# Loading the slots' z rows two slots ahead of their residual rows in a routed feed-forward block

## Chip, cores and metric

The kernel runs on one core of one Trainium2 chip. The metric is device time in microseconds (us) of one execution. The median of three runs of the kernel before is 1089.14 us (1087.94 to 1089.94).

## The reference

A macaron block on x of shape (2, 2048, 256), float32: a routed feed-forward at half weight, causal attention with one head of 128, and the same feed-forward once more.

```python
x = x + 0.5 * ffn(layernorm(x))
x = x + attention(layernorm(x))
x = x + 0.5 * ffn(layernorm(x))
# in ffn, after its gated attention-like part:
h = ln(x, ln2_w, ln2_b)
winners = argmax(bids(h), axis=-1)             # one of 3 experts per token
hr = square(relu(h @ K_rwkv[e]))               # experts 0 and 1, hidden width 1024
out_rwkv = hr @ V_rwkv[e]
out_trans = (h @ W1 * sigmoid(state @ W2)) @ W3   # expert 2
return x + onehot(winners) . all_out * scale
```

## The kernel before

The 4096 tokens go through each feed-forward in two parts. Part A (`ffn_a_*`) takes them in 8 groups of 512: norms, gates, bids, the ranking of the tokens by expert, and expert 2. It writes one row of 514 words per token into a table in device memory, `routed_rows`, at the place that the ranking gives it: 256 words z (the normalized input of the experts), the token's index, 256 words of residual, a gate. GpSimd does this with indirect DMAs, "scatters". For the last two groups each row is scattered in halves (`scatter_half`, L863): the first half holds z and the index, the second, "late" half the residual and the gate. In the first feed-forward GpSimd issues the four late scatters of the last group (L901 to L904, `last_halves`, called at L1471) only after it has done slot 0's subtractions; in the second feed-forward they come before slot 0.

Part B (`ffn_b_*`) reads the table in 17 slots of 256 rows (`NSLOT` = 17), each slot with the weights of expert 0 or 1. For slot j:

- SyncE loads z into `slot_z` (256 KB) and the rest of the rows into `slot_row` (258 KB). There are two buffers of each, used in turn (p = j % 2).
- TensorE transposes z with 8 small matmuls: T(j), L1227. ScalarE copies the result to `shT_hi` (L1325), VectorE subtracts to get `shT_lo` (L1376). Both are needed by the first product, K(j), 48 matmuls of L407 into `bank` 1 to 4 (36 of them are shown as `bank`, 12 as `banks4to`).
- ScalarE takes relu (L1336) and square (L1344, `hr_hi`), VectorE squares in full precision (L1385, `relu_squared`), GpSimd subtracts (L1451, `hr_lo`), four quarters each.
- V(j), 48 matmuls of L407 into `banks4to`, needs all four quarters of `hr_lo` and, for j > 0, that VectorE has finished the output rows of slot j-1.
- VectorE writes `slot_out` from V(j) and `slot_row` (L1392, L1394; semaphore `orow`), and GpSimd scatters it to the output (L1459).

TensorE's order is T(0), T(1), K(0), K(1), T(2), V(0), K(2), T(3), V(1), K(3), T(4), V(2) and so on (`first` and `body`, L1275 to L1286). VectorE's order inside a slot is: bias of slot j+1 (L1367, L1370), the four squares of slot j, `shT_lo` of slot j+1, output rows of slot j-1. Every engine runs its list in order.

SyncE's order is written out in `ffn_b_sync`. It waits until all scatters but the late ones have landed (L1174), loads z of slots 0 and 1 (L1184), waits for the late halves (L1185), loads the rest of slots 0 and 1 (L1187), and then takes slots 2 to 16 one by one with `slot_in`: wait for T(j-2) to be done, load z(j) (L1179), wait until the output rows of slot j-2 are written (`orow` at least j-1, L1180), load the rest (L1181).

After the first feed-forward all engines meet at a barrier; attention and the second feed-forward follow.

Of the kernel before, what the change touches and what calls it, by code (L numbers as in the profile page):

```python
# [20 lines left out]
BATCH, SEQ, C = 2, 2048, 256  # L21
# [10 lines left out]
NSLOT = N // SLOT + 1  # L32
ROWS = NSLOT * SLOT
ROW = 2 * C + 2
# [17 lines left out]
def hold(eng, sem, value, carrier):  # L52

    if isinstance(value, int) and value <= 0:
        return
    eng.wait_ge(sem, value)
    apart(eng, carrier, value)


def apart(eng, carrier, value):  # L60

    if not isinstance(value, int):
        eng.sem_inc(carrier, 1)


def build_kernel(nc, x, w256, w_st, k_w, v_w, w_qkv, ln, shares, ident, tri, mask, tok, slot_row, pad, out):
    with ExitStack() as ctx:
# [166 lines left out]
        @block.sync  # L234
        def _(sp):
            groups = [one.rearrange("(g t p) c -> g p t c", t=GT, p=P) for one in src]
            setup_sync(sp, b, s, s.ffn[0], groups[0], (ln, ident, w256, w_st, tri, mask, shares, tok, slot_row), pad, b.routed[0])
            ffn_a_sync(sp, b, s.ffn[0], groups[0], s, pad, b.routed[0])
            late_sync(sp, b, s, s.ffn[0], k_w, v_w, w_qkv)
            ffn_b_sync(sp, b, s.ffn[0], b.routed[0])  # L240
            barrier(sp, 1)
            attention_sync(sp, b, a, s.cleared, s.ffn[1], groups[1], pad, b.routed[1])
            ffn_a_sync(sp, b, s.ffn[1], groups[1])
            ffn_b_sync(sp, b, s.ffn[1], b.routed[1])
# [926 lines left out]
def ffn_b_sync(sp, b, f, routed):  # L1171
    c = b.carry["sp"]
    for p in range(2):
        sp.wait_ge(f["scat"][p], 16 * GT * NG // 2)  # L1174
    rg = routed.rearrange("(j t p) c -> j p t c", t=ST, p=P)

    def slot_in(j, p):
        hold(sp, f["sT"], j - 1, c)
        sp.dma_start(b.sz[p][:], rg[j][:, :, 0:C]).then_inc(f["s_in"][p], 16)  # L1179
        hold(sp, f["orow"], j - 1, c)  # L1180
        sp.dma_start(b.srow[p][:, :, 0:ROW - C], rg[j][:, :, C:ROW]).then_inc(f["r_in"][p], 16)  # L1181

    for j in range(2):
        sp.dma_start(b.sz[j][:], rg[j][:, :, 0:C]).then_inc(f["s_in"][j], 16)  # L1184
    sp.wait_ge(f["late"], 16 * GT * 2)  # L1185
    for j in range(2):
        sp.dma_start(b.srow[j][:, :, 0:ROW - C], rg[j][:, :, C:ROW]).then_inc(f["r_in"][j], 16)  # L1187
    with sp.Fori(0, (NSLOT - 3) // 2) as it:
        for par in range(2):
            slot_in(it * 2 + 2 + par, par)  # L1190
    slot_in(NSLOT - 1, 0)

def slots(eng, first, body):
# [910 lines left out]
```

## Time and profile before

| | us |
|---|---|
| median of 3 runs | 1089.14 |
| profiled execution, its own time | 1091.29 |
| its span in the profile | 1089.5 |
| TensorE busy in the span | 1000.6 (92%) |
| TensorE's weight loads busy | 919.8 (84%) |
| VectorE / ScalarE / GpSimd busy | 691.2 / 564.8 / 496.5 |
| mean granted TensorE clock | 0.97 of full |

Slots run from 206.9 to some 437 us in the first feed-forward and from 870 us to the end in the second. In the views, PE is TensorE, PEld its weight loads, DVE VectorE, ACT ScalarE, POOL GpSimd, SPq the queue of SyncE. A timeline row gives start, length, engine, line, operation, what it writes and reads, and in brackets how long the engine stood idle before it and for whom. PEclk is the granted TensorE clock as a share of 2.4 GHz, so 0.50 is 1.2 GHz.

### The profile page before, as it was taken

How to read it: one execution, taken by the hardware profiler on the slowest of the kernel's cores; microseconds unless marked ns; L12 is line 12 of the kernel's file. 1: busy time of each engine (PE TensorE's matmuls, PEld its weight loads, DVE VectorE, ACT ScalarE, POOL GpSimd, SP SyncE). 2: the span in 40 equal slices, each digit the busy share in tenths (PEclk: the TensorE clock that was granted, in tenths of full speed). 3: DMA queues.
4: the chain of work that ended last, by engine and by line, in shares of the span. 5: the costliest groups of instructions: out<-in, count | busy, mean ns of one | idle time of the engine just before them, and what ended most of it. 6: DMA issues, size and time to landing. Idle time of an engine off the chain costs nothing.

```text
span 1089.5 us, 21438 instructions
## 1 busy us (share of the span) xinstructions
PE 1000.6 (92%) x7076; PEld 919.8 (84%) x7077; DVE 691.2 (63%) x1750; ACT 564.8 (52%) x1185; POOL 496.5 (46%) x541
## 2 busy tenths in 40 slices
PE   8999998959999999889988899899999699999997
PEld 7788886959999999778887788678888599999997
DVE  5688877836555554456765668578887764555553
ACT  5776655434454443245553555676664264444552
POOL 3254634456566556551221001135634576556665
PEclk8999998779999999999999999999999799999999
DMA  8621243122111111310222233402212222112211
GB/s 269 200 95 67 90 136 136 59 63 75 59 48 58 58 59 59 100 37 11 87 98 87 78 117 127 145 20 102 75 40 79 78 79 61 58 48 68 77 59 41
DMA packets 51845, 90.01 MB, mean 83 GB/s; under 512 B 5902, under 2 KB 44176, under 8 KB 50576
## 3 DMA queue, kind: packets, MB, share of 16 engines
q1 hardware_dynamic: 43120, 63.64, 18.7%
q0 software_dynamic: 8640, 25.24, 6.2%
q8 instruction: 52, 0.85, 0.3%
q14 instruction: 33, 0.27, 0.1%
HBM read 59.44 MB, written 47.85 MB: 98 GB/s over the span
## 4 chain that ended last, share of the span: by engine, by line
PE 66%; DVE 16%; DMA 6%; ACT 5%; issue 4%; POOL 3%; SPq 1%; DVEq 0%; POOLq 0%; ACTq 0%
PE banks4to L407 32%; PE bank L407 22%; PE banks4to L1694 3%; DMA slot_z<-routed_rows 2%; DVE out_rows L1053 2%; DVE pT_lo L1955 2%; PE bank L1227 2%; PE bank L503 1%; DVE gT_lo L955 1%; PE bank L1706 1%; DVE zT_lo L944 1%; DVE chunk_max L1945 1%; DMA attn_x<-x_after_ffn 1%; PE bank L371 1%; DMA routed_rows<-out_rows,row_index 1%
## 5 line engine op out<-in xcount | busy, mean ns | idle before, releaser
L1385 DVE TENSOR_TENSOR relu_squared<-relu 128x512 f32<-128x512 f32 x136 | 154.9, 1153 | 105.7 <-ACT relu L1336 55.3
L1451 POOL TENSOR_TENSOR hr_lo<-relu_squared,hr_hi 128x512 fp32r<-128x512 f32 x136 | 188.4, 1398 | 59.8 <-DVE relu_squared L1385 55.3
L1336 ACT ACTIVATE relu<-bank,slot_k_bias 128x256 f32<-128x256 f32 x204 | 84.8, 467 | 185.4 <-PE bank L407 168.0
L407 PE MATMUL banks4to<-v_hi,hr_hi 128*128 128x256 f32 x544 | 156.6, 288 | 3.7 <-DVE slot_out L1394 3.0
L407 PE MATMUL banks4to<-v_hi,hr_lo 128*128 128x256 f32 x544 | 153.3, 282 | 0.0
L407 PE MATMUL banks4to<-v_lo,hr_hi 128*128 128x256 f32 x544 | 153.3, 282 | 0.0
L407 PE MATMUL bank<-shT_hi,k_hi 128*128 128x256 f32 x408 | 116.9, 287 | 8.2 <-issue 5.4
L407 PE MATMUL bank<-shT_lo,k_hi 128*128 128x256 f32 x408 | 115.2, 282 | 0.0
L407 PE MATMUL bank<-shT_hi,k_lo 128*128 128x256 f32 x408 | 114.9, 282 | 0.0
L407 PEld LDWEIGHTS banks4to<-v_hi,hr_hi 128*128 128x128 f32 x544 | 103.5, 190 | 7.5 <-issue 7.0
L407 PEld LDWEIGHTS banks4to<-v_hi,hr_lo 128*128 128x128 f32 x544 | 103.5, 190 | 0.0
L407 PEld LDWEIGHTS banks4to<-v_lo,hr_hi 128*128 128x128 f32 x544 | 103.3, 190 | 0.0
L880 POOL DMA_INDIRECT routed_rows<-out_rows,row_index x48 | 48.1, 1001 | 117.6 <-DVE row_index L1036 106.6
L1344 ACT ACTIVATE hr_hi<-relu 128x512 fp32r<-128x512 f32 x136 | 86.1, 633 | 15.9 <-ACT relu L1336 6.9
L407 PEld LDWEIGHTS bank<-shT_hi,k_hi 128*128 128x128 f32 x408 | 76.9, 188 | 11.9 <-issue 11.5
L407 PEld LDWEIGHTS bank<-shT_hi,k_lo 128*128 128x128 f32 x408 | 76.9, 188 | 0.0
L407 PEld LDWEIGHTS bank<-shT_lo,k_hi 128*128 128x128 f32 x408 | 76.6, 188 | 0.0
L1840 ACT CAST pT_hi<-bank 128x512 fp32r<-128x512 f32 (+1 forms) x72 | 39.2, 564 | 55.1 <-PE bank L1706 54.9
L1831 ACT ACTIVATE p<-banks4to,minus_row_max 128x512 f32<-128x512 f32 (+2 forms) x80 | 49.8, 629 | 29.5 <-DVE minus_row_max L1948 18.0
L1459 POOL DMA_INDIRECT x_after_ffn<-slot_out,token_index x32 | 32.7, 1023 | 62.5 <-DVE slot_out L1394 57.6
L1955 DVE TENSOR_TENSOR pT_lo<-bank,pT_hi 128x512 fp32r<-128x512 f32 (+1 forms) x72 | 46.2, 658 | 22.2 <-ACT pT_hi L1840 21.8
L1392 DVE COPY token_index<-slot_row 128x2 int32<-128x2 int32 x32 | 5.7, 177 | 82.4 <-PE banks4to L407 82.4
(279 smaller groups left out, 3031.7 us busy)
## 6 DMA issues: line engine op xcount, KB each, us to landing
routed_rows<-in_pad SPq DMA_DIRECT2D x34, 514.0 KB, 5.2
slot_row<-routed_rows SPq DMA_DIRECT2D x34, 258.0 KB
slot_z<-routed_rows SPq DMA_DIRECT2D x34, 256.0 KB
attn_x<-x_after_ffn SPq DMA_DIRECT2D x16, 256.0 KB, 2.9
attn_out<-x_after_ffn SPq DMA_DIRECT2D x16, 256.0 KB, 2.7
x_after_attention<-attn_out SPq DMA_DIRECT2D x16, 256.0 KB, 2.1
x_rows<-x_after_attention SPq DMA_DIRECT2D x8, 512.0 KB, 5.1
x_rows<-in_x SPq DMA_DIRECT2D x7, 512.0 KB, 4.0
```

The costliest lines, as they stand in the source:

```text
L407: mm = pe.matmul(outv, w(pw), m(pm), start=(n_first and k == 0), stop=(n_last and k == 2))
L880: pool.indirect_dma_start(routed, bass.IndirectOffsetOnAxis(b.posi[g % 2][:, t:t + 1].bitcast(U32), 0), b.rows[g % 2][:, t, :], None).then ...
L1053: last = dve.scalar_tensor_tensor(rows[:, t, RES], b.bank(6 + t // 2)[:, (t % 2) * C:(t % 2 + 1) * C], b.gt[p][:, t:t + 1], rows[:, t, RES ...
L1336: last = act.activation(b.r[q % 2][:, (h % 2) * SLOT:(h % 2 + 1) * SLOT], b.bank(1 + q)[:, (h % 2) * SLOT:(h % 2 + 1) * SLOT], ACT.Relu, b ...
L1344: act.activation(b.hr[p][0][:, 2 * q:2 * q + 2].rearrange("p h n -> p (h n)"), b.r[q % 2][:, :], ACT.Square).then_inc(f["hrhi"], 1)
L1385: dve.tensor_tensor(b.sq[q % 2][:, :], b.r[q % 2][:, :], b.r[q % 2][:, :], ALU.mult).then_inc(f["sq"], 1)
L1451: pool.tensor_tensor(b.hr[p][1][:, 2 * q:2 * q + 2].rearrange("p h n -> p (h n)"), b.sq[q % 2][:, :], b.hr[p][0][:, 2 * q:2 * q + 2].rearr ...
L1459: pool.indirect_dma_start(dst, bass.IndirectOffsetOnAxis(b.idx[p][:, t:t + 1].bitcast(U32), 0), b.o[p][:, t, :], None, bounds_check=N - 1, ...
L1694: mm = pe.matmul(out[:, at:at + n], b.kq[pw][:, q, 0, t * P:(t + 1) * P], part, start=(k == 0 and i == 0 and not last), stop=(k == 2), ski ...
L1831: act.activation(b.p[s % 2][t][:, c * KEYS:c * KEYS + w], bank(("S", s, t, c))[:, 0:w], ACT.Exp, bias=b.nbias[:, s % 2, t:t + 1], accum_ou ...
L1840: act.copy(b.pT[m % 2][0][:, 0:w], b.bank(m % 2)[:, 0:w]).then_inc(a["pthi"], 1)
L1955: dve.tensor_tensor(b.pT[m % 2][1][:, 0:w], b.bank(m % 2)[:, 0:w], b.pT[m % 2][0][:, 0:w].bitcast(F32), ALU.subtract).then_inc(a["ptlo"], 1)
```

## The change

`slot_in` is split in two: `z_in(j)` (wait for T(j-2), load z) and `row_in(j)` (wait for the output rows of slot j-2, load the rest). The list becomes: z of slots 0 to 3; wait for the late halves; rows of slots 0 and 1; then row(2), z(4), row(3), z(5), and so on to row(14), z(16), row(15), row(16). The buffers, the waits in front of each load, the number of loads and all other engines' programs are the same. The loop makes 6 passes instead of 7.

```diff
-    def slot_in(j, p):
+    def z_in(j, p):
         hold(sp, f["sT"], j - 1, c)
         sp.dma_start(b.sz[p][:], rg[j][:, :, 0:C]).then_inc(f["s_in"][p], 16)
+
+    def row_in(j, p):
         hold(sp, f["orow"], j - 1, c)
         sp.dma_start(b.srow[p][:, :, 0:ROW - C], rg[j][:, :, C:ROW]).then_inc(f["r_in"][p], 16)
 
-    for j in range(2):
-        sp.dma_start(b.sz[j][:], rg[j][:, :, 0:C]).then_inc(f["s_in"][j], 16)
+    for j in range(4):
+        z_in(j, j % 2)
     sp.wait_ge(f["late"], 16 * GT * 2)
     for j in range(2):
-        sp.dma_start(b.srow[j][:, :, 0:ROW - C], rg[j][:, :, C:ROW]).then_inc(f["r_in"][j], 16)
-    with sp.Fori(0, (NSLOT - 3) // 2) as it:
+        row_in(j, j)
+    with sp.Fori(0, (NSLOT - 5) // 2) as it:
         for par in range(2):
-            slot_in(it * 2 + 2 + par, par)
-    slot_in(NSLOT - 1, 0)
-
+            row_in(it * 2 + 2 + par, par)
+            z_in(it * 2 + 4 + par, par)
+    row_in(NSLOT - 3, 0)
+    z_in(NSLOT - 1, 0)
+    row_in(NSLOT - 2, 1)
+    row_in(NSLOT - 1, 0)
```

## Rows read from the trace of the kernel before

**Rows 1.** TensorE's waits, first feed-forward's slots (206-436 us): us in total, times, longest

```profile
PE bank L1227 <- DMA slot_z<-routed_rows: 13.0, 4, 11.5
```

**Rows 2.** TensorE's waits, second feed-forward's slots (865-1087 us)

```profile
PE bank L1227 <- DMA slot_z<-routed_rows: 1.2, 2, 0.9
```

**Rows 3.** Timeline of TensorE, 190-300 us: start, us, engine, line, out<-in, [idle before <-releaser]

```profile
206.93 0.79 PE L1227 MATMUL bank<-ident_sb,slot_z 128*128 128x128 f32 x4
...
220.81 0.28 PE L407 MATMUL banks4to<-shT_lo,k_hi 128*128 128x256 f32 x1
232.54 1.11 PE L1227 MATMUL bank<-ident_sb,slot_z 128*128 128x128 f32 x4 [11.46 <-DMA slot_z<-routed_rows]
...
241.19 0.28 PE L407 MATMUL bank<-shT_hi,k_hi 128*128 128x256 f32 x1
```

**Rows 4.** Timeline of SyncE's DMA issues, 190-300 us

```profile
227.86 0.88 SPq L1187 DMA_DIRECT2D slot_row<-routed_rows  x2
```

**Rows 5.** The chain that ended last, 195-300 us: start, us, what

```profile
229.19 3.31 DMA slot_z<-routed_rows
...
233.66 7.72 PE banks4to L407 x48
...
243.23 4.57 DMA slot_z<-routed_rows
...
247.84 0.66 PE bank L1227 x4
248.50 5.63 PE banks4to L407 x48
...
254.51 4.55 PE bank L407 x36
```

**Rows 6.** Timeline of GpSimd, 190-300 us

```profile
218.04 2.88 POOL L1451 TENSOR_TENSOR hr_lo<-relu_squared,hr_hi 128x512 fp32r<-128x512 f32 x2 [0.69 <-DVE relu_squared L1385]
...
226.23 2.49 POOL L1451 TENSOR_TENSOR hr_lo<-relu_squared,hr_hi 128x512 fp32r<-128x512 f32 x2
229.42 2.80 POOL L1451 TENSOR_TENSOR hr_lo<-relu_squared,hr_hi 128x512 fp32r<-128x512 f32 x2 [0.70 <-DVE relu_squared L1385]
```

**Rows 7.** Timeline of VectorE, 205-256 us

```profile
218.43 1.27 DVE L1367 TENSOR_SCALAR slot_k_bias_part<-k_bias,slot_expert 128x8 f32<-128x8 f32 x1
...
227.61 2.27 DVE L1385 TENSOR_TENSOR relu_squared<-relu 128x512 f32<-128x512 f32 x2 [5.45 <-POOL hr_lo L1451]
```

**Rows 8.** Timeline of VectorE, second feed-forward

```profile
888.72 0.68 DVE L1376 TENSOR_TENSOR shT_lo<-bank,shT_hi 128x512 fp32r<-128x512 f32 x1
```

**Rows 9.** Timeline of GpSimd, second feed-forward

```profile
888.34 2.89 POOL L1451 TENSOR_TENSOR hr_lo<-relu_squared,hr_hi 128x512 fp32r<-128x512 f32 x2 [0.70 <-DVE relu_squared L1385]
```

**Rows 10.** Timeline of TensorE, attention stage: two idle stretches

```profile
487.90 0.66 PE L1653 MATMUL banks4to<-ident_sb,attn_x 128*128 128x128 f32 x4 [2.36 <-ACT p L1831]
...
582.36 0.39 PE L407 MATMUL bank<-wao_hi,oT_hi 128*128 128x256 f32 x1 [2.96 <-DVE oT_lo L1960]
```

**Rows 11.** Stretches: us, busy us of PE, PEld, DVE, ACT, POOL, then PEclk, DMA share, GB/s

```profile
488.00:492.00 4.00, 3.78 (x22) 2.82 (x23) 1.64 (x3) 2.33 (x7) 0.00 (x0) 1.00 0.00 0
582.00:586.00 4.00, 3.58 (x16) 3.28 (x17) 3.27 (x10) 0.46 (x2) 3.40 (x4) 0.60 0.01 4
```

**Rows 12.** Timeline of TensorE, second feed-forward, 880-900 us

```profile
884.52 0.66 PE L1227 MATMUL bank<-ident_sb,slot_z 128*128 128x128 f32 x4
...
890.65 0.28 PE L407 MATMUL bank<-shT_hi,k_hi 128*128 128x256 f32 x1
...
897.43 0.65 PE L1227 MATMUL bank<-ident_sb,slot_z 128*128 128x128 f32 x4 [0.87 <-DMA slot_z<-routed_rows]
```

**Rows 13.** Timeline of SyncE's DMA issues, second feed-forward

```profile
866.38 0.89 SPq L1184 DMA_DIRECT2D slot_z<-routed_rows  x2
879.74 0.88 SPq L1187 DMA_DIRECT2D slot_row<-routed_rows  x2
```

**Rows 14.** SyncE's waits over the whole span: us in total, times, longest

```profile
SPq L1187 <- DMA routed_rows<-out_rows,half_row_index: 41.0, 2, 28.5
```

## The prediction

> **What bounds the kernel now.** The page gives TensorE 92% of the span, so a change to loads can only win where TensorE stands still for one. I asked for TensorE's waits in the two stretches that the change touches. In the first feed-forward's slots it waits four times for `slot_z`, 13.0 us, of which one wait is 11.5 us [rows 1]; in the second, twice, 1.2 us [rows 2]. That is 14.2 us, the most that removing these waits alone could give, but for the clock.
>
> Next, TensorE's timeline around the long wait. T(0) starts at 206.93, the last matmul of K(1) at 220.81, T(2) only at 232.54, and K(2) at 241.19 [rows 3]. SyncE's issues say why: it stood at the wait for the late halves and loaded the rows of slots 0 and 1 only at 227.86 [rows 4]; z(2), whose buffer had been free since T(0), came behind them at 229.19 and landed 3.31 us later [rows 5]. V(0) stands behind T(2) in TensorE's list, so it waited too, though its inputs were ready when GpSimd ended slot 0's subtractions at 218.04 + 2.88 = 220.92 [rows 6]. z(3) is asked at 243.23, after slot 0's output rows, and lands 4.57 us later, just before T(3) at 247.84 [rows 5].
>
> **The change, part by part.** *z(2) and z(3) in the first feed-forward.* They wait for T(0) and T(1), so they go out at about 208 to 209. Loads of this size took 3.31 and 4.57 us [rows 5]; they are in by 214, seven us before TensorE wants the first. T(2) then starts where K(1) ends, 220.81 + 0.12 = 220.93. The second feed-forward has the same code without a wait there: from T(2) at 884.52 to K(2) at 890.65 are 6.13 us [rows 12]. TensorE is through with V(0) at 227.1.
>
> *What is late next.* K(2) needs `shT_lo` of slot 2, which VectorE makes after slot 1's four squares. Their last two run from 227.61 for 2.27 us, to 229.88, because they wait for GpSimd, which issues the late scatters first and reaches slot 1's subtractions at 226.23 [rows 6, 7]. The change touches none of this. So `shT_lo`, 0.68 us [rows 8], ends at 230.56, and K(2) starts at 230.65: 10.54 us sooner. This takes in the faster V(0) (7.72 us at a low clock against 5.63 at a full one [rows 5]), and is less than the wait because 227.1 to 230.65, some 3.5 us, is a new idle stretch. Bounds: not before 229.88, as the squares end there (0.7 us more gain), and not after 231.5, below.
>
> A rule to weigh here. VectorE's bias step beside GpSimd's subtractions took 1.27 us [rows 7], so the two engines do get in each other's way. But the very instruction in question ran in 0.68 us at 888.72, inside GpSimd's pair of 888.34 to 891.23 [rows 8, 9]. I take 0.68. If it had to wait out the first subtraction of the pair at 229.42 (2.80 / 2 = 1.40 us [rows 6]), it would run 230.82 to 231.50, and the gain would be 0.9 us less; that is the upper end above. The Trainium skill, "SBUF — State Buffer", section "SBUF: two separate sides", states that the port pair which VectorE and GpSimd share is an exclusive lock for a whole instruction, for VectorE operations with two SBUF inputs or in a two-port mode. By the lock the sum would lose that 0.9 us; by its exemption, one of this instruction's inputs being in PSUM, it loses nothing, and the trace agrees.
>
> *The clock.* Does the new idle stretch cost speed behind it? After 2.36 us of idle TensorE came back at full clock, after 2.96 us it did not [rows 10]: PEclk was 1.00 in 488 to 492 and 0.60 in 582 to 586 [rows 11]. A stretch of 3.5 us is on the far side. The loss is (1 - 0.60) x 4 us = 1.6 us, laid on K(2), which nothing covers. Bounds: nothing, if the clock holds; 2.1 us, what V(0) lost behind the long wait (7.72 - 5.63 [rows 5]). I take 1.6, the row nearest in length.
>
> *T(3).* K takes 890.65 to 896.56 in the second feed-forward (T(3) starts at 897.43 after 0.87 of wait [rows 12]), 5.91 us. So K(2) ended at 247.10 and T(3) waited 0.74 us. z(3) is now there: 0.74 gained.
>
> *The other slots.* SyncE's steady pattern was row(j-1), z(j) behind the output rows of slot j-3; it is now row(j-1), z(j+1) behind the same event, since the wait for T(j-1) is over by then. One row load and one z load leave together as before, at the same moments; only each z is a whole slot (K and V, some 12 us) earlier for its user. The other waits vanish: 13.0 - 11.46 - 0.74 = 0.8 us here [rows 1, 3] and 1.2 us in the second feed-forward, where 0.87 is T(3)'s [rows 2, 12]. TensorE is the bound there, so they count in full. Bounds: 0 to 2.0.
>
> *At nothing:* the split into two functions and one loop pass less move only SyncE's own bookkeeping; that engine waits for nearly all of the slots. Loads in number and size are the same. The row loads of slots 0 and 1 go out at 227.86 as before, and the z load issued behind them was in by 232.50 [rows 4, 5], so they were about in by then too. Output rows of slot 0 then end at about 233.5. V(1) asks for them after K(2) and T(3), at 237.2 or later: 3.7 us of cover. If that went, V(1) would start late by the excess.
>
> **Sum:** 10.54 + 0.74 + 0.8 + 1.2 - 1.6 = 11.7 us. The profiled execution took 1091.29 us around a span of 1089.5; by the same steps it becomes 1079.6. It is 2.15 us over the median, which is taken to fall by the same amount: 1089.14 - 11.7 = 1077.4 us.
>
> **Rivals.** *B, the clock holds over the new idle stretch* (or falls too late to matter). The two idle stretches of attention had thin work around them, while this one has dense matmuls on both sides; against it is that 3.5 us is longer than the 2.96 that brought the fall [rows 10]. Gain 13.3, time 1075.8. Chance 0.33.
>
> *C, VectorE and GpSimd become the bound for another slot.* Slot 0's output rows and scatter used to come when they had nothing else; now they come nearer to K(2)'s quarters, about 1 us later against its start. If slot 2's squares slip behind a pair of subtractions (2.89 us [rows 9]), K(3) waits by up to that. For it: in slots 0 to 3 the two engines' chain, not TensorE, is what I find limiting at 227 to 230. Against: before the change K(3) followed without such a wait. Time 1077.4 + 2.9 = 1080.3. Chance 0.12.
>
> *D, no change:* z loads are early, but something I don't see keeps T(2) or V(0) where it is, for instance a wait of the same place hidden under the 11.46 us. The second feed-forward runs the same list with no wait there [rows 12], which speaks against it. Time 1089. Chance 0.04.
>
> *E, slower: the early z loads hold up the late scatters in the second feed-forward.* There T(0) and T(1) are done at about 871, so z(2) and z(3) go out just as GpSimd issues the last late halves; the late wait ended at 879.74 [rows 13]. Slot 0's rows would be in at 884.3 (4.57 us [rows 5]) and its output rows written at 885.4; V(1) wants them at 897.2. So nothing happens until the late halves are 11.8 us late, and the kernel is slower only from 11.8 + 11.7 (the gain of the sum) = 23.5 us. If they took as long as SyncE's longest such wait, 28.5 us more [rows 14], the loss would be 28.5 - 11.8 = 16.7 against the gain of 11.7: 1089.14 + 5.0 = 1094.1. Two loads of 4.6 us hardly do that. Chance 0.03. The Trainium skill, "DMA: Bandwidth & Descriptors", section "Queues, rings and completion order", says that each DMA engine goes round between the queues that have work, packet by packet. By it the scatters would be slowed by some us but not shut out, which the slack takes; no run here shows it yet.
>
> **How the numbers follow.** The remaining 0.48 is the forecast's. Low end: B, less 1.0 us for how far a median of three can lie from the true one (the runs span 2.0 us): 1074.8. High end: C and 0.7 more for the bounds of `shT_lo` and of the clock: 1081.0. That holds the forecast, B and C, 0.93 by their chances; some of that is for terms I have not seen. About 0.2% (2.2 us) is what a measurement of this kernel can tell from no change. Faster by more than that: forecast, B and C, 0.93; within it: D, 0.04; slower: E, 0.03.
>
> **What would show it.** In the first feed-forward: SyncE's third and fourth z loads at about 208, before the wait for the late halves; T(2) at 220.9 with no idle before it; V(0) in about 5.6 us; an idle stretch of about 3.5 us before K(2), released by `shT_lo`, not by a DMA; K(2) near 230.65, with PEclk near 0.5 for some 3 us from there if the forecast is right and 1.00 if B is; K(3) 9.7 us earlier than 254.51 [rows 5], so near 244.8 (243.2 under B). TensorE's waits for `slot_z` are gone in both feed-forwards. The row loads of slots 0 and 1 stay at 227.86. I am wrong if T(2) still waits for `slot_z`, if V(1) waits for output rows, if K(3) waits for more than 1 us on `shT_lo` or a relu, or if SyncE's late wait in the second feed-forward ends more than 11 us later against T(2) than before.

## The result and the profile after

The changed kernel takes 1070.29 us (median of 4 runs, 1068.25 to 1072.83) against 1088.54 for the kernel before (4 runs, 1087.36 to 1089.94): a ratio of 0.9833 with a 95% interval of 0.9808 to 0.9858, 18.25 us faster. The forecast was 11.7 us faster, 1077.4, in a range of 1074.8 to 1081.0. The sign and the chain of events at the front came as forecast. What the later slots would give did not, and the time lies below the range.

The page of the changed kernel, its first lines. TensorE's busy time fell by 8.9 us and the span by 21.2, so 12.3 us of idle time went:

```profile
span 1068.3 us, 21420 instructions
...
PE 991.7 (93%) x7076; PEld 915.2 (86%) x7077; DVE 691.4 (65%) x1750; ACT 565.0 (53%) x1185; POOL 496.7 (46%) x541
```

The timeline of SyncE's DMA issues, 190 to 275 us, in answer to [rows 4] (rows of one line close together are merged, with the time from the first start to the last end):

```profile
195.52 9.94 SPq L1179 DMA_DIRECT2D slot_z<-routed_rows  x4
224.54 4.79 SPq L1183 DMA_DIRECT2D slot_row<-routed_rows  x3
229.69 0.38 SPq L1179 DMA_DIRECT2D slot_z<-routed_rows  x1
```

Four z loads are out by 205.46, nineteen us ahead of the first row load.

The timeline of TensorE, 202 to 229 us, in answer to [rows 3]:

```profile
203.95 0.60 PE L1232 MATMUL bank<-ident_sb,slot_z 128*128 128x128 f32 x4
...
217.63 0.28 PE L407 MATMUL banks4to<-shT_lo,k_hi 128*128 128x256 f32 x1
217.76 0.60 PE L1232 MATMUL bank<-ident_sb,slot_z 128*128 128x128 f32 x4
218.11 0.36 PE L407 MATMUL banks4to<-v_hi,hr_hi 128*128 128x256 f32 x1
...
223.71 0.28 PE L407 MATMUL banks4to<-v_lo,hr_hi 128*128 128x256 f32 x1
227.50 0.57 PE L407 MATMUL bank<-shT_hi,k_hi 128*128 128x256 f32 x1 [3.51 <-DVE shT_lo L1381]
```

T(2) follows K(1) without a gap, V(0) runs at full speed, and the new idle stretch before K(2) is 3.51 us, released by `shT_lo`. Stretches of the trace behind it, in answer to [rows 11]:

```profile
227.00:231.00 4.00, 3.50 (x17) 3.51 (x18) 2.38 (x6) 0.49 (x2) 2.12 (x2) 0.57 0.35 98
231.00:235.00 4.00, 4.00 (x36) 4.00 (x36) 1.39 (x2) 3.82 (x9) 3.03 (x3) 1.00 0.34 109
```

The granted clock is near half for the first part of K(2), then full. TensorE's waits in the first feed-forward's slots (206 to 425 us), in answer to [rows 1]: no wait for `slot_z` is left.

```profile
PE bank L407 <- DVE shT_lo L1381: 4.7, 2, 3.5
PE bank L407 <- issue: 2.6, 6, 0.6
PE banks4to L407 <- DVE slot_out L1399: 1.5, 1, 1.5
PE bank L1320 <- POOLq L228: 0.7, 1, 0.7
```

**Where the time went.** I cut the traces at five marks in TensorE's timeline: T(0), K(3) and V(15) of the first feed-forward, then the same of the second. Two profiles of the kernel before and three of the changed one (the second and third come from the runs below), in us:

| stretch | before | changed | mean difference | forecast |
|---|---|---|---|---|
| start to T(0) | 206.93, 204.34 | 203.95, 205.61, 203.73 | 1.2 | 0 |
| T(0) to K(3) | 47.58, 46.80 | 37.49, 37.50, 37.40 | 9.7 | 9.7 |
| K(3) to V(15) | 168.82, 167.91 | 164.21, 164.45, 164.51 | 4.0 | 0.8 |
| V(15) to the second T(0) | 447.03, 447.77 | 447.69, 447.44, 446.80 | 0.1 | 0 |
| second T(0) to K(3) | 33.78, 32.68 | 32.71, 32.59, 32.34 | 0.7 | 0.9 |
| second K(3) to V(15) | 167.57, 168.13 | 164.50, 164.32, 164.34 | 3.5 | 0.3 |
| to the end of the span | 17.79, 17.84 | 17.79, 17.78, 17.84 | 0.0 | 0 |

The whole surprise sits in two rows: slots 4 to 16 of both feed-forwards, 7.5 us where the sum had 1.1.

**How a wait hides.** T of a slot is four transposes (x4 in the rows), not the eight told ahead of the prediction. The kernel before, timeline of TensorE, 360 to 374 us, at T(12):

```profile
360.80 0.28 PE L407 MATMUL banks4to<-shT_lo,k_hi 128*128 128x256 f32 x1
361.09 0.63 PE L1227 MATMUL bank<-ident_sb,slot_z 128*128 128x128 f32 x4
361.79 0.39 PE L407 MATMUL banks4to<-v_hi,hr_hi 128*128 128x256 f32 x1
```

The changed kernel at the same T(12), 344 to 360 us:

```profile
345.51 0.29 PE L407 MATMUL banks4to<-shT_lo,k_hi 128*128 128x256 f32 x1
345.64 0.60 PE L1232 MATMUL bank<-ident_sb,slot_z 128*128 128x128 f32 x4
345.99 0.36 PE L407 MATMUL banks4to<-v_hi,hr_hi 128*128 128x256 f32 x1
```

In the second, T begins 0.13 us after the start of K's last matmul, and V 0.35 us after T. In the first it is 0.29 and 0.70 us: half a us more. Yet no bracket marks an idle stretch. One part is hidden by the drawing: a matmul is drawn 0.28 us long where the next can start 0.12 us after it, so a wait of up to 0.16 us lies under the drawn length, and the views leave out what sticks out by less than 0.15 us. The other part lies between T and V. TensorE's weight loads at the same two places, the kernel before first:

```profile
361.06 0.42 PEld L1227 LDWEIGHTS bank<-ident_sb,slot_z 128*128 128x128 f32 x4 [0.18 <-issue]
361.79 0.19 PEld L407 LDWEIGHTS banks4to<-v_hi,hr_hi 128*128 128x128 f32 x1 [0.32 <-issue]
```

```profile
345.53 0.47 PEld L1232 LDWEIGHTS bank<-ident_sb,slot_z 128*128 128x128 f32 x4
345.97 0.19 PEld L407 LDWEIGHTS banks4to<-v_hi,hr_hi 128*128 128x128 f32 x1
```

The transposes themselves are no slower (0.63 and 0.60 us in all), but in the kernel before V's first product starts 0.35 us after the last of them and not 0.03 us after it. No semaphore that the profile shows ends this gap. In TensorE's program the waits for `hr_lo` and for the output rows and the branch on the slot's expert stand there; that they are passed in advance when z is early would fit, but no run shows it.

The measure that catches both parts is start to start: from K(j)'s first matmul to V(j-1)'s. It is 6.18 us (6.11 in slot 15) in every later slot of the changed kernel, 80.3 us for K(3) to K(15). In the kernel before it runs from 6.18 to 7.25 us, in sum 84.56 and 83.50 in the two profiles of the first feed-forward and 83.30 and 84.04 in the second: 3.0 to 4.3 us over. The waits view showed 0.8 and 0.34 of that. Of the 7.3 and 6.9 us that each profile has over in both feed-forwards, 2.7 and 2.3 lie before T and 4.2 and 4.3 between the last transpose and V.

### The profile page after: what moved, and what is told of

It is laid out like the page before. It is cut to its first block, busy times and chain, and to the rows that moved or that the text cites. A ratio compares the mean times of both kernels' runs of the same rounds, so it can differ in the third digit from the quotient of the medians.

```text
span 1068.3 us, 21420 instructions
## 1 busy us (share of the span) xinstructions
PE 991.7 (93%) x7076; PEld 915.2 (86%) x7077; DVE 691.4 (65%) x1750; ACT 565.0 (53%) x1185; POOL 496.7 (46%) x541
## 4 chain that ended last, share of the span: by engine, by line
PE 67%; DVE 17%; ACT 5%; issue 4%; POOL 3%; DMA 3%; SPq 0%; DVEq 0%; POOLq 0%; ACTq 0%
PE banks4to L407 32%; PE bank L407 25%; PE banks4to L1699 3%; DVE out_rows L1053 2%; DVE pT_lo L1960 2%; DVE gT_lo L955 1%; PE bank L1711 1%; PE bank L503 1%; DVE zT_lo L944 1%; PE bank L1232 1%; DMA attn_x<-x_after_ffn 1%; DVE chunk_max L1950 1%; PE bank L493 1%; DMA routed_rows<-out_rows,row_index 1%; POOL attn_x L2053 1%
## 5 line engine op out<-in xcount | busy, mean ns | idle before, releaser
L407 PE MATMUL bank<-shT_hi,k_hi 128*128 128x256 f32 x408 | 117.8, 289 | 11.7 <-DVE shT_lo L1381 6.1
L838 POOL TENSOR_SCALAR rsqrt_work<-mean_var 128x4 f32<-128x4 f32 x16 | 3.3, 208 | 116.4 <-DVE mean_var L922 115.6
```

The source lines that it names most:

```text
L407: mm = pe.matmul(outv, w(pw), m(pm), start=(n_first and k == 0), stop=(n_last and k == 2))
```

## The experiments

The kernel before has medians from 1087.4 to 1089.1 us in the measurements; each ratio is against its executions beside the same runs. Each diff is against the changed kernel and shortened, with "..." where lines are left out. The theory, A: z of nearly every later slot came some tenths of a us late. The rivals (with letters of their own, not those of the prediction), B: the surplus came from the clock or the stages behind; D: it came from a load landing beside its user's work.

### Only the first two z early

```diff
     sp.wait_ge(f["late"], 16 * GT * 2)
-    for j in range(2):
-        row_in(j, j)
+    for j in range(3):
+        row_in(j, j % 2)
     with sp.Fori(0, (NSLOT - 5) // 2) as it:
         for par in range(2):
-            row_in(it * 2 + 2 + par, par)
+            row_in(it * 2 + 3 + par, 1 - par)
             z_in(it * 2 + 4 + par, par)
...
```

> Only z(2) and z(3) are loaded early; from slot 4 on each z leaves behind the row load of the slot before, as in the kernel before. Theory A (z of nearly every later slot came a little late, in waits that the waits view doesn't list): gain over before = 9.9 us to K(3) in the first feed-forward and 1.1 us at T(3) in the second, 11.0, so about 1077.5 us; from a K's start to the next V's start is 6.2 to 7.2 us in slots 4 to 15 as before, with a sum some 7 us over 6.18 each, over both feed-forwards. Rival B (the unforeseen 6.5 us come from a changed clock or from the stages behind, not from the later slots' z): about 1070 to 1072 us. The record's own sum (0.8 and 0.34 us of waits in the later slots) gives 1078.5 and can't be told from A here.

Measured: 1073.64 us, ratio 0.9878 (0.9858 to 0.9898), 15.0 us faster. K(2) waits 3.5 us for `shT_lo` as in the changed kernel, and the first feed-forward's K(3) comes 37.51 us after T(0). K to V is 83.34 us in the first feed-forward and 81.36 in the second: 3.0 and 1.1 over 80.3. So the hidden waits are there, but 4.1 us together against some 7.1 in the kernel before. That makes 3.0 of the 3.9 us by which it beat A's number and came near B's; the rest stays open. My edit had moved the turn of SyncE's loop as well; the run after the next two tests that.

### Only the later z early

```diff
-    for j in range(4):
-        z_in(j, j % 2)
+    for j in range(2):
+        z_in(j, j)
     sp.wait_ge(f["late"], 16 * GT * 2)
     for j in range(2):
         row_in(j, j)
+    for j in range(2, 4):
+        z_in(j, j % 2)
```

> z(2) stays behind the late halves as before, z(3) and all later z come ahead of their rows as in the changed kernel. Theory A: gain = 4.3 + 3.0 us of hidden waits in slots 4 to 16 and 0.9 + 1.1 at T(3), 9.2 us, so about 1079.3 us; every K to V from slot 4 on takes 6.18 us. The record's sum: 0.74 + 0.8 + 1.2 = 2.7 us, about 1085.8. Rival B: near 1088.5, as this leaves the long wait where it was. The wait of some 11.5 us before T(2) stays in all.

Measured: 1080.22 us, 0.993 (0.9917 to 0.9943), 8.4 us faster with the long wait in place. TensorE's waits, 200 to 430 us:

```profile
PE bank L1234 <- DMA slot_z<-routed_rows: 11.7, 1, 11.7
```

One wait of 11.7 us is listed, against four of 13.0 in all before [rows 1], but K to V is 6.18 or 6.19 in every slot from 3 on, 80.35 us. B, which had no gain here, falls, and so does the recorded sum of 2.7 us. A's own number, 9.2 us, was 0.8 too high.

### Of each pair, z first

```diff
...
-    with sp.Fori(0, (NSLOT - 5) // 2) as it:
+    z_in(2, 0)
+    with sp.Fori(0, (NSLOT - 3) // 2) as it:
         for par in range(2):
+            hold(sp, f["orow"], it * 2 + 1 + par, c)
+            z_in(it * 2 + 3 + par, 1 - par)
             row_in(it * 2 + 2 + par, par)
-            z_in(it * 2 + 4 + par, par)
...
```

(and z(2), z(3) after the late halves, as before the change)

> The kernel before, but of the two loads that leave together behind the output rows of slot j-3, z(j) goes first and the rest of slot j-1 second; z leads by some 0.65 us more than before and no longer stands behind 258 KB. Theory A (z was late by tenths of a us): this alone takes nearly all of the 9.2 us, about 1079 to 1081 us, with K to V at 6.18 us in nearly all slots. Rival D (what helps is that a load no longer lands beside its user's transposes or products, by contention, not by lateness): under 2 us of gain, about 1087.

Measured: 1079.77 us, 0.9925 (0.9911 to 0.9939), 8.9 us faster. SyncE's issues, 250 to 268 us:

```profile
251.32 0.37 SPq L1179 DMA_DIRECT2D slot_z<-routed_rows  x1
251.94 0.38 SPq L1183 DMA_DIRECT2D slot_row<-routed_rows  x1
```

Moving z by one place in a pair, 0.62 us and 258 KB, takes K to V to 80.35 and 80.47 us. Both loads still land in the same slot, so D falls. The two-slot lead is not needed for this part.

### The same order, the loop's turn elsewhere

```diff
...
     for j in range(2):
         row_in(j, j)
-    with sp.Fori(0, (NSLOT - 5) // 2) as it:
+    z_in(2, 0)
+    with sp.Fori(0, (NSLOT - 3) // 2) as it:
         for par in range(2):
             row_in(it * 2 + 2 + par, par)
-            z_in(it * 2 + 4 + par, par)
+            z_in(it * 2 + 3 + par, 1 - par)
...
```

(the order of loads of the kernel before)

> The order of loads of the kernel before, unchanged, but SyncE's loop pass begins with row(j) instead of z(j), so its turn (in the trace of before 1.0 to 1.2 us between row(odd) and the next z, against 0.63 within a pass) no longer lies between a row load and the z that follows it. Theory A (z is late by tenths of a us, so each tenth of lead counts): half of the later z leave about 0.45 us sooner, and the later slots' waits fall from 7.3 us to some 4 us, as in the run with only the first two z early: gain about 3 us, 1085.5. Rival D (not lateness but contention, or the number of loads in flight): no gain, 1088.6. The long wait stays.

Measured: 1085.15 us (12 runs), 0.9975 (0.996 to 0.9991), 2.2 us faster. The kernel before, SyncE's issues, 255 to 310 us:

```profile
255.34 0.37 SPq L1181 DMA_DIRECT2D slot_row<-routed_rows  x1
256.44 0.28 SPq L1179 DMA_DIRECT2D slot_z<-routed_rows  x1
268.28 0.37 SPq L1181 DMA_DIRECT2D slot_row<-routed_rows  x1
268.91 0.37 SPq L1179 DMA_DIRECT2D slot_z<-routed_rows  x1
```

This kernel, 250 to 281 us:

```profile
251.78 0.38 SPq L1183 DMA_DIRECT2D slot_row<-routed_rows  x1
252.42 0.37 SPq L1179 DMA_DIRECT2D slot_z<-routed_rows  x1
264.70 0.37 SPq L1183 DMA_DIRECT2D slot_row<-routed_rows  x1
265.33 1.20 SPq L1179 DMA_DIRECT2D slot_z<-routed_rows  x1
```

Before, the step from row to z is 1.10 us at the loop's turn shown here (0.96 to 1.18 over both feed-forwards) and 0.63 within a pass; here it is 0.64 and 0.63. K to V falls to 81.86 and 82.57 us, 3.8 over in sum against 7.1. What is left sits in the other slots: at T(4), T(6) and so on to T(14), whose z now leave 0.3 to 0.5 us sooner after their row, the surplus falls from 3.6 and 3.1 us in the two profiles of the kernel before to 0.05 us; at T(5) to T(15), whose step is as before, it stays, 3.8 us against 3.7 and 3.9. The kernel with only the first two z early has the loop's turn at the same place, and the same pattern, 0.7 and 3.5 us. So the surplus follows the lead slot by slot, within one execution. The 2.2 us of the median are less than the 3.3 us of K to V; the profiled execution took 1081.68 us where the twelve run from 1081.36 to 1087.30, and its stretch from V(15) to the second T(0), which this edit does not touch, was 444.87 us against 446.3 to 449.8 in all other profiles.

### The kernel before once more

> The kernel before once more, for the spread: no difference in time, within 0.2%. Its profile shows whether T(0) of the first feed-forward comes at 206.9 us as in the first profile of this kernel, or near 203.9 as in four other profiles; if it differs between profiles of one kernel, the 3.2 us by which the changed kernel's trace was ahead at T(0) are the clock's luck in code that the change doesn't touch.

Measured: 1087.72 us (10 runs), 1.001 (0.9995 to 1.0026). Timeline of TensorE, 203 to 206 us:

```profile
204.34 0.60 PE L1227 MATMUL bank<-ident_sb,slot_z 128*128 128x128 f32 x4
```

T(0) at 204.34 against 206.93 in [rows 3]. The 3.0 us by which the changed kernel's first profile was ahead at T(0) are thus no gain of the change; the median difference, 18.25, is the number to explain, not the 21.2 of the two first profiles.

This trace, and that of the run above, also has the landing of every z load. The z loads of the first feed-forward's later slots (L1179), this kernel first:

```profile
DMA to landing us min/median/max: 2.8/3.3/3.8
DMA to landing us min/median/max: 2.8/2.9/3.9
```

Set against the moment when T could have started (0.12 us after the start of K's last matmul), the landings make A more exact. Of the 52 z loads of the later slots in the two traces, 48 landed before that moment, so most z were not late by that measure, and still cost time:

| z landed ahead of T's earliest start | loads | last transpose to V, us |
|---|---|---|
| 0.70 us or more | 15 | 0.03 |
| 0.55 to 0.70 | 7 | 0.03 to 0.15 |
| 0.42 to 0.55 | 13 | 0.03 to 0.24 |
| 0.30 to 0.42 | 6 | 0.20 to 0.37 |
| 0 to 0.30 | 7 | 0.21 to 0.39 |
| after it | 4 | 0.21 to 0.31, and T itself waits |

Only with 0.7 us or more in hand did z never cost anything in these traces.

### Taking the new idle stretch away

VectorE makes `shT_lo` of slot 2 after two of slot 1's squares:

```diff
...
-        sq(j, p)
+        early = isinstance(j, int) and j == 1
+        sq(j, p, range(2 if early else HC // 2))
         if not last:
             slo(j + 1, 1 - p)
+        if early:
+            sq(j, p, range(2, HC // 2))
```

> The changed kernel, and VectorE makes shT_lo of slot 2 after the first two squares of slot 1 instead of after all four, so K(2) no longer waits for GpSimd's late scatters. If that chain is what holds K(2) (3.51 us idle before it in the changed kernel) and the low clock follows from that idle stretch: K(2) starts where V(0) ends, PEclk stays at 1.00, gain over the changed kernel 3.5 + about 1.6 = 5 us, about 1065.5 us. If the idle stretch costs no clock: 3.5 us, about 1067. Rival: V(1) then waits for slot 0's output rows, whose row load leaves at about 224.5 in the trace's time, and gives it back: 0 to 2 us of gain, with TensorE idle before V(1).

Measured: 1070.05 us, 0.9835 (0.9818 to 0.9852): nothing over the changed kernel. K(2) has no idle stretch ahead of it, as expected. Timeline of TensorE, 236 to 243 us:

```profile
242.09 0.55 PE L407 MATMUL bank<-shT_hi,k_hi 128*128 128x256 f32 x1 [2.98 <-DVE shT_lo L1381]
```

and VectorE at that place, 214 to 250 us:

```profile
238.69 2.28 DVE L1390 TENSOR_TENSOR relu_squared<-relu 128x512 f32<-128x512 f32 x2 [4.77 <-POOL hr_lo L1459]
240.89 0.68 DVE L1381 TENSOR_TENSOR shT_lo<-bank,shT_hi 128x512 fp32r<-128x512 f32 x1
```

The stall moved on by one slot: V(1) did not wait for output rows, as my rival had it, but K(3) for `shT_lo`, behind squares that waited for GpSimd. And the slow clock came behind that stretch (PEclk 0.50 from 242 to 248 us): K(3) to V(2) took 8.88 us against 6.18. K(3) came 34.99 us after T(0), 2.5 us sooner than in the changed kernel, and the 2.7 us lost behind it ate that up. That is rival C of the prediction, in another kernel.

The same for slots 2 and 3 (`j <= 2`):

> As the run that made shT_lo of slot 2 early, and the same for slot 3 (shT_lo after two squares in slots 1 and 2). That run moved the stall from K(2) to K(3): 3.0 us idle before K(3), released by shT_lo, because GpSimd's backlog held slot 2's last squares, and a low clock behind it. If the backlog is worn off by slot 4, both stalls are gone: K(3) about 32.3 us after T(0) instead of 37.5, PEclk 1.00, 5 us faster than the changed kernel, about 1065.3. Rival: the stall moves on to V(2) or K(4), since GpSimd still has the same work: 1068 to 1070.

Measured: 1066.17 us, 0.9809 (0.9787 to 0.9832). Stretches of this kernel (columns as in [rows 11]), 218 to 236 us:

```profile
218.00:224.00 6.00, 6.00 (x54) 6.00 (x53) 1.56 (x3) 3.31 (x7) 5.06 (x5) 1.00 0.26 90
224.00:230.00 6.00, 6.00 (x52) 6.00 (x52) 5.09 (x9) 2.83 (x6) 4.38 (x4) 1.00 0.31 91
230.00:236.00 6.00, 5.76 (x49) 5.56 (x47) 1.92 (x3) 3.31 (x7) 4.08 (x4) 1.00 0.43 134
```

No idle stretch, full clock, K(3) 32.21 us after T(0) against 37.49. In every slot (`early = not last`):

> shT_lo of the next slot after two squares in every slot but the last. If the backlog of GpSimd moves a stall on from slot to slot, this one takes it in every slot: about 1065. Rival: in the steady slots VectorE now stands waiting for ScalarE's shT_hi before its third square, GpSimd gets late and V waits: 0.3 us or more per slot, 1075 or more.

Measured: 1065.26 us, 0.9792 (0.9772 to 0.9812). K(3) 32.30 us after T(0), K to V at 80.3 in both feed-forwards, so VectorE's wait for `shT_hi` costs TensorE nothing.

Both forms and the changed kernel again, each form measured beside the changed kernel:

> The changed kernel once more, beside the one with early shT_lo: the time of the first measurement (1070.3) within 1.5 us if nothing but the clock's luck moves it. From K to V 6.18 us in all later slots again; K(2) again about 3.5 us after V(0), and slower by some 1.5 us wherever a low-clock stretch follows at once.

Measured: 1070.14 us, 0.9825 (0.9802 to 0.9847).

> Early shT_lo in every slot once more, to set it against the changed kernel with the same executions of the kernel before: if the 5 us idle and low clock before and in K(2) were what it takes away, 4 to 5.5 us less than the changed kernel. Rival: the difference of the earlier calls was spread, and they are within 2 us.

Measured: 1068.60 us, 0.9803 (0.978 to 0.9827), only 1.5 us below its neighbour.

> Early shT_lo for slots 2 and 3 only, beside the changed kernel in one call. The form with early shT_lo in every slot won 5.0 us from T(0) to K(3) in the trace, but only 1.5 us in the median against the changed kernel, and both its profiles show a low clock of 10.2 us at the start of attention where the changed kernel has 3.4. If that is luck: 4 us less than the changed kernel here. If the early form brings it by itself: 1 to 2.5 us less, with 6.8 us or more of low clock there.

Measured: 1067.50 us, 0.9801 (0.9782 to 0.982).

> The changed kernel for the comparison in the same call: 1070 us within 1.5; T(0) of the first feed-forward between 203.7 and 207.1 us, K(3) 37.5 us behind it whatever T(0) is, low clock of 3.4 us at the start of attention.

Measured: 1068.75 us, 0.9836 (0.9819 to 0.9852), 1.25 us above its neighbour. Over all runs, the two-slot form has a median of 1066.2 (10 runs), the every-slot form 1066.4 (10) and the changed kernel 1070.1 (14 runs): about 4 us, but the two pairs measured side by side gave 1.3 and 1.5 (3.1 and 2.7 by their means). Side by side, all five runs of the two-slot form (1064.1 to 1068.2) lie below all five of the changed kernel (1068.2 to 1071.1). Of the 5.2 us won at K(3) some come back later: from V(15) to the second T(0) the four early profiles take 448.8 to 449.8 us, the changed kernel's three 446.8 to 447.7. PEclk of 420 to 444 us, the start of attention, was 0.93 in all three profiles of the changed kernel, 0.86 in both of the two-slot form and 0.79 in both of the every-slot form. Cut at the same distance behind V(15) it comes out the same: 3.4, 6.8 and 10.2 us at the low clock. That it is the same in both profiles of a form speaks for the form as its cause, but the kernels with only the later z early and with z first, which make no `shT_lo` early, had 6.8 us there too and took 448.8 and 448.4 us to the second T(0). The mechanism stays open. The early forms beat both kernels, the changed one by 1 to 4 us.

## Why the prediction was right and wrong

**Right: the front.** K(3) came 9.7 us sooner against T(0), as the sum had it (10.54 + 0.74 - 1.6). Each link is in the trace: T(2) without idle; V(0) at 5.7 us (5.6 forecast); 3.51 us idle, estimated at some 3.5; K(2) released by `shT_lo`, 23.55 us after T(0), where the sum had 230.65 - 206.93 = 23.7. Taking 0.68 us for `shT_lo` beside GpSimd's pair was right, too: it ran in 0.68 us at 226.66 inside the pair of 226.28 to 229.12. The Trainium skill, "SBUF — State Buffer", section "SBUF: two separate sides", names the lock only for VectorE operations with two SBUF inputs or in a two-port mode. This one has one input in PSUM, and these numbers agree.

**Right: the clock.** It fell at the end of the idle stretch in all three profiles of the changed kernel: K(2) to V(1) took 7.63, 7.70 and 7.61 us, 6.11 at full clock, so 1.5 to 1.6 us against the 1.6 taken. Rival B did not happen.

**Right: the second feed-forward's T(3)** in size, 0.7 for 0.87. It varies: in the second profile of the kernel before T(3) did not wait, and T(2) did, 0.4 us. Rival E did not happen: there the row loads of slots 0 and 1 left 863.21 - 853.34 = 9.9 us after T(0), against 879.74 - 870.36 = 9.4 before. C did not happen in this kernel, and D not.

**Wrong: the other slots.** The step that failed said "The other waits vanish: 0.8 us here and 1.2 us in the second feed-forward", of which 0.34 in the later slots, with bounds of 0 to 2.0. The later slots gave 4.0 and 3.5 us. I had taken the waits view as complete, and it lists only what sticks out beyond the drawn length of a matmul; the larger part, between the last transpose and V, I had not looked for. The mechanism, z moved out of TensorE's way, was right, and its size was not. It was open to be seen: z(5), for one, left at 268.91, 2.5 us after V(2) was through, and landed 3.70 us later, 6.2 us in all. In the same time TensorE went from V(2) to K(4) (0.2 us here, 0.1 to 0.8 elsewhere) and through K(4) (5.83 us), 6.0 us. With such a balance near zero in all 26 later slots, a view that reports 3 of them should have been suspected. Since the bounds were read off the same view, the range was too narrow by the same error. With 7.5 for 1.1 in the sum, it gives 18.1 us, and 18.25 was measured.

The Trainium skill, "DMA: Bandwidth & Descriptors", section "Anatomy of one DMA — SWDGE (gpsimd) path", gives 2.0 us plus the bytes over 436 GB/s for one DMA of GpSimd's path, by which 256 KB would take, as an estimate, 2.6 us. The z loads here, issued by SyncE right behind a row load, took 2.8 to 4.6 us, and the measurement decides. By 2.6 us every later z of the kernel before would have landed 0.7 us or more ahead of T, where the table above has no loss.

## What to carry to other kernels

When a load is due about when its user is, measure the user's period start to start over all repetitions and compare it with the shortest one; a waits view built on modelled matmul ends leaves out waits of a few tenths of a us, which 26 slots turn into 7 us. A load can cost time though it lands before its user could start: here it had to be in 0.7 us ahead. In a queue that issues in order, the place of the urgent load within a pair was worth as much as a whole slot of lead (8.9 against 8.4 us), and that of the loop's turn 2 to 3 us. When a wait is removed, look at which engine's backlog it covered: here GpSimd's, which moved the stall to K(2), and once that was mended, to K(3).

## What was new of the hardware

- A loop's turn on SyncE put 0.3 to 0.5 us between two DMA issues (0.96 to 1.18 against 0.63 us), enough to show in the kernel's time (2.2 us over two feed-forwards).
- A load that landed less than 0.7 us before TensorE could start on it delayed TensorE by up to 0.4 us in a place behind its first use, between the last transpose and the next product, with no wait listed. Why is not shown.
- Before any changed instruction, T(0) came between 203.7 and 207.1 us in different profiles of kernels with the same code there. PEclk of 172 to 207 us was 0.80 in seven profiles, with T(0) at 203.7 to 204.3, 0.76 in one (203.8) and 0.71 in six (204.4 to 207.1). A single pair of profiles can thus differ by 3 us before the change has begun.
- Idle stretches of 2.98 and 3.51 us before dense matmuls were both followed by the 1.2 GHz level (PEclk 0.50), as the 2.96 us of [rows 10] was; the cost was 1.5 us after 3.51 us and 2.7 us after 2.98.
